# VectorE in place of TensorE for turning two weight matrices: WV ahead of step 0, Wo within it

## The reference, cut to what matters

```python
x = x + (x @ W.T + adapter_b(x @ A_b.T))          # layer 0, adapter by sequence
x = x + einsum('bct,bcd->bdt', x, w1[idx1])       # layer 1, mixes tokens
# layer 2, attention
q, k, v = x @ Wq.T, x @ Wk.T, x @ Wv.T            # per head of 32; q scaled by beta
attn = softmax(where(causal, q @ k.T / sqrt(32), min))
x = x + (attn @ v) @ Wo.T
x = x + einsum('bct,bcd->bdt', x, w3[idx3])       # layer 3, mixes tokens
```

## Time and profile before

| | us |
|---|---|
| median of 3 runs | 619.65 (619.6 to 620.12) |
| the profiled execution | 619.72 |
| its span, first to last instruction | 618.0 |
| TensorE busy in the span | 604.5 (98%) |
| VectorE busy | 386.8 (63%) |
| ScalarE busy | 225.0 (36%) |
| GpSimd busy | 109.7 (18%) |

### The profile page before, as it was taken

The page is one execution under the profiler, slowest core; times in us unless marked ns, Lnnn a source line. Parts: engine busy times, 40 slices in busy tenths (PEclk is TensorE's granted clock), DMA queues, the critical chain, the costliest instruction groups (busy, mean ns, idle before and its releaser), DMA issues.

```text
span 618.0 us, 21481 instructions
## 1 busy us (share of the span) xinstructions
PE 604.5 (98%) x8534; PEld 522.7 (85%) x8534; DVE 386.8 (63%) x561; ACT 225.0 (36%) x434; POOL 109.7 (18%) x101
## 2 busy tenths in 40 slices
PE   6999999899999999999999999999999999999998
PEld 5897979789898888989888898988989788898885
DVE  3569676565766756576675757666575765637374
ACT  4534533242434425143342514435152442413222
POOL 2004030120303003030310303021030302203030
PEclk9999999899999999999999999999999999999999
DMA  8541313222232222223222222323223222220212
GB/s 276 168 146 48 90 43 83 73 50 70 72 88 72 60 72 63 72 76 93 68 64 72 62 74 72 76 74 79 72 57 79 72 64 73 60 73 5 69 41 103
DMA packets 62104, 48.29 MB, mean 78 GB/s; under 512 B 16826, under 2 KB 47546, under 8 KB 62074
## 3 DMA queue, kind: packets, MB, share of 16 engines
q1 hardware_dynamic: 58122, 41.84, 24.9%
q10 hardware_dynamic: 3952, 6.03, 2.9%
HBM read 30.54 MB, written 17.30 MB: 77 GB/s over the span
## 4 chain that ended last, share of the span: by engine, by line
PE 95%; DVE 1%; DMA 1%; issue 1%; ACT 1%; ACTq 0%; DVEq 0%
PE banks L617 10%; PE banks L622 10%; PE banks L618 10%; PE banks L645 5%; PE banks L716 5%; PE banks L717 5%; PE banks L723 5%; PE banks L647 5%; PE banks L649 5%; PE banks L557 5%; PE banks L559 5%; PE banks L561 5%; PE banks L670 4%; PE banks L662 4%; PE banks L686 3%; PE banks L601 3%
## 5 line engine op out<-in xcount | busy, mean ns | idle before, releaser
L617 PE MATMUL banks<-x1T_hi,w_hi 128*128 128x256 f32 x512 | 130.3, 287 | 0.2 <-ACT x_in L885 0.2
L618 PE MATMUL banks<-x1T_hi,w_lo 128*128 128x256 f32 x512 | 128.2, 283 | 0.0
L617 PEld LDWEIGHTS banks<-x1T_hi,w_hi 128*128 128x128 f32 x512 | 98.0, 191 | 0.8 <-ACT x_in L885 0.4
L618 PEld LDWEIGHTS banks<-x1T_hi,w_lo 128*128 128x128 f32 x512 | 98.1, 192 | 0.0
L1374 POOL TENSOR_TENSOR probs<-probs,row_max 128x1024 f32<-128x1024 f32 x32 | 61.0, 1906 | 123.5 <-DVE row_max L1176 123.5
L622 PE MATMUL banks<-x1T_lo,w_hi 128*128 128x256 f32 x512 | 82.2, 283 | 0.0
L1356 POOL TENSOR_TENSOR w_own<-w_in,own 128x128 f32<-128x128 f32 x32 | 14.7, 460 | 361.4 <-PE banks L584 267.4
L622 PEld LDWEIGHTS banks<-x1T_lo,w_hi 128*128 128x128 f32 x512 | 70.6, 192 | 0.0
L1162 DVE TENSOR_TENSOR qkT<-banks,beta 128x512 f32<-128x512 f32 x32 | 22.1, 690 | 61.7 <-PE banks L622 61.7
L885 ACT ACTIVATE x_y<-banks 128x512 f32<-128x512 f32 (+1 forms) x17 | 9.9, 584 | 128.8 <-PE banks L584 122.0
L1180 DVE TENSOR_REDUCE row_sum<-probs 128x16 f32<-128x1024 f32 x32 | 39.0, 1218 | 24.2 <-ACT probs L966 24.2
(11 more groups left out here) (133 smaller groups left out, 1055.3 us busy)
## 6 DMA issues: line engine op xcount, KB each, us to landing
x_rows<-x_in SPq DMA_DIRECT2D x64, 128.0 KB, 2.3
x_kept<-x_rows SPq DMA_DIRECT2D x16, 512.0 KB, 3.7
x_in<-in_x_dram SPq DMA_DIRECT2D x60, 128.0 KB, 2.8
out_dram<-x_y SPq DMA_DIRECT2D x15, 512.0 KB, 3.0
b_sel<-b_parts SPq DMA_DIRECT2D x180, 32.0 KB, 1.7
w_in<-in_L_cond_weights_dram SPq DMA_DIRECT2D x128, 16.0 KB
probsT<-in_L_cond_W_dram ACTq DMA_DIRECT2D x1, 1024.0 KB, 7.3
probs<-in_L_cond_Wk_dram ACTq DMA_DIRECT2D x1, 1024.0 KB, 5.9
```

The costliest lines, as they stand in the source:

```text
L617: nc.tensor.matmul(out_ap, w_hi[:, w, c, cols], x1T_hi[:, c, :], start=(c == 0), stop=False)
L618: nc.tensor.matmul(out_ap, w_lo[:, w, c, cols], x1T_hi[:, c, :], start=False, stop=False)
```

## The change

WV and WO are loaded in 32-row blocks with four DMAs each (`load_blocks`, rows of 512 bytes) and turned by VectorE (`turn_w(n)`, eight parts of 128x512) into a new SBUF tile `w_whole` of four parts. Parts 0 to 3 are WV, 4 to 7 WO. ACT copies a part to `w_hi` (`part_hi`), VectorE subtracts into `w_lo` (`part_lo`). TensorE's eight `turn_part` calls for them are gone, and it waits for `part_split` ahead of `values(0, 0)` (4) and of `scores(1)` (8). WV's load is issued after W0's parts and WO's after WV's part 2. In step 0, `query_part(0)` goes ahead of the keys. For WO's new layout `attend` writes head `4m+j` to partitions `32m` of chunk `j` (before, partitions `32j` of chunk `m`), with the two loops exchanged, in all steps.

```diff
+        w_whole = sb("w_whole", [P, NC, NC, P])
...
-                 WV: as_stage(probsT[:], "p t (c d) -> p (t c) d"),
-                 WO: x2_y[:].rearrange("p a t d -> p (a t) d")}
+                 WV: probsT[:].rearrange("p t n -> p (t n)").rearrange("p (b n) -> p b n", n=P),
+                 WO: x2_y[:].rearrange("p a t d -> p (a t d)").rearrange("p (b n) -> p b n", n=P)}
...
-        GROUPS_OF = {W0: range(0, 4), WK: range(6, 10), WQ: range(10, 14), WV: range(14, 18), WO: range(18, 22)}
-        ring = [0, 6, 7, 4, 5, 6, 7, 4, 5, 6, 0, 7, 6, 7, 6, 7, 6, 7, 0, 5, 6, 7]
+        GROUPS_OF = {W0: range(0, 4), WK: range(6, 10), WQ: range(10, 14)}
+        ring = [0, 6, 7, 4, 5, 6, 7, 4, 5, 6, 0, 7, 6, 7]
...
+        PARTS_V, PARTS_O = range(NC), range(NC, 2 * NC)
+
+        def matrix_part(w, n):
+            k = WV if n in PARTS_V else WO
+            return w[:, k, :, n % NC * P:(n % NC + 1) * P]
+
+        def whole_part(n):
+            return w_whole[:, n % NC]
...
             def attend():
                 for t in range(TILES):
-                    for m in range(NC):
+                    for j in range(JG):
                         for r in range(SEQT):
-                            for j in range(JG):
+                            for m in range(NC):
                                 at = j % 2 * BANK + (m // 2 * TILES + t) * P + m % 2 * S
                                 head = (JG * m + j) * HD
                                 last = nc.tensor.matmul(
-                                    attn_bank(r)[j * HD:(j + 1) * HD, m, t, :], v[half(r), t, head:head + HD],
+                                    attn_bank(r)[m * HD:(m + 1) * HD, j, t, :], v[half(r), t, head:head + HD],
...
+                    pe.wait_ge(part_split, len(PARTS_V))
...
                     pe.wait_ge(v_copied, TILES)
                     adapters_down(2)
-                    turn_part(WO, 0)
+                pe.wait_ge(x1_hi_done, TILES * (i + 2))
+
+                if not prev:
+                    query_part(0, split=TILES * 2)
                 pe.wait_ge(x1_copied, SEQT * i + 1)
-                pe.wait_ge(x1_hi_done, TILES * (i + 2))
                 for m in range(NC):
                     if m == 2:
                         pe.wait_ge(x1_copied, SEQT * (i + 1))
                     key_part(i + 1, m)
-                    if not prev and m > 0:
-                        if m == 1:
-                            pT_copied(0, HG)
-                        turn_part(WO, m)
-                if not prev:
-                    pe.wait_ge(turned_lo, GROUPS_OF[WO][0] + 1)
-                for m in range(NC):
+                for m in range(NC) if prev else range(1, NC):
                     if m == 2:
                         pe.wait_ge(k_copied_act, i + 2)
                     if m == (1 if parted(i) else 3):
                     pe.wait_ge(y_copied_act, i)
                     pe.wait_ge(y_copied_dve, i)
...
-                    pe.wait_ge(turned_lo, GROUPS_OF[WO][-1] + 1)
+                    pe.wait_ge(part_split, len(PARTS_V) + len(PARTS_O))
...
             turn_part(WQ, 3)
-            turn_part(WV, 0)
             pe.wait_ge(x1_hi_done, TILES)
             for m in range(NC):
                 key_part(0, m)
-                if m == 0:
-                    pe.wait_ge(tables_done, PSEQ)
-                else:
-                    turn_part(WV, m)
+            pe.wait_ge(tables_done, PSEQ)
             pe.wait_ge(turned_lo, GROUPS_OF[WQ][-1] + 1)
             for m in range(NC):
                 if m == 2:
                     pe.wait_ge(k_copied_act, 1)
                 query_part(m)
-            pe.wait_ge(turned_lo, GROUPS_OF[WV][-1] + 1)
             adapters_down(1)
...
+            def load_blocks(k, matrix):
+                for g in range(JG):
+                    act.dma_start(stage[k][g * SQ:(g + 1) * SQ],
+                                  matrix.rearrange("(b j) (g n) -> g j b n", j=SQ, g=JG)[g]).then_inc(w_loaded[k], 16)
...
                     xa_low_part(2)
-                    take_hi(GROUPS_OF[WO][0], w_hi[:, WO, 0, :])
+                    xa_hi_part(2)
+                    for n in PARTS_O:
+                        part_hi(n)
                     copy_k(1)
-                    for c in range(1, NC):
-                        take_hi(GROUPS_OF[WO][c], w_hi[:, WO, c, :])
-                    xa_hi_part(2)
                 if nxt2:
...
+            def part_hi(n):
+                act.wait_ge(part_turned, n + 1)
+                copy(matrix_part(w_hi, n), whole_part(n)).then_inc(part_hi_done, 1)
...
             take_matrix(W0)
+            load_blocks(WV, Wv)
             take_hi(GROUP_A, a_all[:, 0:2, :], in_chunks(bank_of_group(GROUP_A))[:, 0:2, :])
...
             copy(xa_first_hi, xa_first).then_inc(xa_first_hi_done, 1)
-            load_w(WV, Wv)
             for c in range(3):
                 take_hi(GROUPS_OF[WK][c], w_hi[:, WK, c, :])
+                part_hi(c)
+            act.wait_ge(xa_first_split, 1)
+            load_blocks(WO, Wo)
             x0_copy(0)
             take_hi(GROUPS_OF[WK][3], w_hi[:, WK, 3, :])
             take_hi(GROUPS_OF[WQ][0], w_hi[:, WQ, 0, :])
...
             take_hi(GROUPS_OF[WQ][3], w_hi[:, WQ, 3, :])
-            load_w(WO, Wo)
-            take_hi(GROUPS_OF[WV][0], w_hi[:, WV, 0, :])
+            part_hi(3)
             x_hi(1)
-            take_hi(GROUPS_OF[WV][1], w_hi[:, WV, 1, :])
             copy_k(0)
-            for c in (2, 3):
-                take_hi(GROUPS_OF[WV][c], w_hi[:, WV, c, :])
             act.wait_ge(turned_lo, GROUP_A + 1)
...
-                    for c in range(NC):
-                        if c == NC - 1:
-                            copy_k(1)
-                        take_lo(GROUPS_OF[WO][c], w_lo[:, WO, c, :], w_hi[:, WO, c, :])
+                    for n in PARTS_O:
+                        turn_w(n)
+                    for n in PARTS_O:
+                        part_lo(n)
+                    copy_k(1)
                 if nxt2:
...
+            def turn_w(n):
+                k, first = (WV, PARTS_V[0]) if n in PARTS_V else (WO, PARTS_O[0])
+                if n == first:
+                    dve.wait_ge(w_loaded[k], 16 * JG)
+                if k == WO:
+                    dve.wait_ge(part_split, n - NC + 1)
+                blocks = stage[k][:, NC * (n - first):NC * (n - first + 1), :]
+                nc.vector.transpose(
+                    whole_part(n).rearrange("p c (b j) -> p b c j", j=SQ),
+                    blocks.rearrange("p b (e c) -> p b c e" if k == WV else "p b (c e) -> p b c e", c=NC))\
+                    .then_inc(part_turned, 1)
+
+            def part_lo(n):
+                dve.wait_ge(part_hi_done, n + 1)
+                rest(matrix_part(w_lo, n), whole_part(n), matrix_part(w_hi, n)).then_inc(part_split, 1)
...
                 take_lo(GROUPS_OF[WK][c], w_lo[:, WK, c, :], w_hi[:, WK, c, :])
+                turn_w(c)
             x0_copy(0)
...
             dve.wait_ge(tables_done, PSEQ)
-            take_lo(GROUPS_OF[WV][0], w_lo[:, WV, 0, :], w_hi[:, WV, 0, :])
+            turn_w(3)
             turn_x(1)
-            for c in (1, 2):
-                take_lo(GROUPS_OF[WV][c], w_lo[:, WV, c, :], w_hi[:, WV, c, :])
+            for n in PARTS_V:
+                part_lo(n)
             copy_k(0)
-            take_lo(GROUPS_OF[WV][3], w_lo[:, WV, 3, :], w_hi[:, WV, 3, :])
             x_lo(1)
             scale_q(0)
             sum_xa(1)
```

More of the change, by code:

```diff
@@ L196, in cond_resid_kernel @@
         tables_done = sem("tables_done")
+        part_turned = sem("part_turned")
+        part_hi_done = sem("part_hi_done")
+        part_split = sem("part_split")
         xT_mm = sem("xT_mm")
@@ L285, in attn_of @@
         def attn_of(ap, r):
-            return ap.rearrange("p m (t b s) -> p b m t s", t=TILES, b=SEQT)[:, r]
+            return ap.rearrange("p j (t b s) -> p b j t s", t=TILES, b=SEQT)[:, r]
         def attn_bank(r):
-            return bank[AT[r]].rearrange("p (m t s) -> p m t s", m=NC, t=TILES)
+            return bank[AT[r]].rearrange("p (j t s) -> p j t s", j=NC, t=TILES)
         def own_blocks(r):
@@ L324, in last_attn @@
         def last_attn(ap, t, r):
-            return ap.rearrange("p m (t b s) -> p m t b s", t=TILES, b=SEQT)[:, :, t, r]
+            return ap.rearrange("p j (t b s) -> p j t b s", t=TILES, b=SEQT)[:, :, t, r]
         def last_attn_bank(t, r):
-            return bank[SC[TILES * t + r]][:, 0:PT].rearrange("p (m s) -> p m s", m=NC)
+            return bank[SC[TILES * t + r]][:, 0:PT].rearrange("p (j s) -> p j s", j=NC)
         HALF_D = D // 2
+        PARTS_V, PARTS_O = range(NC), range(NC, 2 * NC)
[4 more added lines that the diff above has]
+            return w_whole[:, n % NC]
         block = ctx.enter_context(nc.Block())
@@ L489, in pieces_of @@
             def pieces_of(k, dc):
-                if k != WO:
-                    return [every_fourth(stage[k][:, oc, :], dc) for oc in range(NC)]
```

(8 more changed lines are left out.)

## The result

Measured beside each other: the kernel after 626.83 us (median of 4 runs, 623.11 to 629.43), before 619.62; ratio 1.0123, 95% interval 1.0095 to 1.0152. The same source measured again gave 626.23 beside 619.79. The forecast was 621.8, the range ended at 624.6: the sign was right, the loss was 7 us, not 2.

What follows compares the result with a forecast made beforehand. TensorE was taken as the bound, busy 604.5 of 618.0 us, so its new waits are paid in full. Terms -1.9 + 4.6 + 1.4 - 1.9 = +2.2 gave 621.8 us, range 620.0 to 624.6.

Steps and rivals of the forecast that it cites:

- term 1: Prologue: TensorE no longer turns WV's four parts, 0.48 us each; -1.9 us.
- term 2: Prologue: `first_layer1` waits for ScalarE's copy of x0, starting at 30.3 in place of 25.73; +4.6 us.
- term 3: Behind the prologue's gap: TensorE's clock falls to the lower level for a stretch; +1.4 us, bounds 0 and 3.4.
- term 4: Step 0 to step 1's values: WO's parts off TensorE, query 0 ahead of the keys; -1.9 us, or -0.8 with slow turns.
- bound 21.8: Prologue: start of VectorE's first WV turn if the queues share badly; 21.0 was taken, not before 20.8.
- a lap: Prologue chain: one turn, ScalarE's parts of WV and WK, and VectorE's subtraction; 2.8 us.
- the issues: Prologue chain: ScalarE's four DMA issues for WO ahead of its copy of x0; 1.8 us.
- two stretches: Within rival "More is paid" (22%, 623 to 624.8): two stretches at the lower clock after the gap, +1.8 us more.
- the clock stays up: Rival, 15%: no clock loss behind the prologue's gap, terms 1, 2 and 4 alone; +0.8, 620.5 us.
- faster: Rival, 13%: TensorE's shorter program removes the 2.0 us stop in step 1's `scores` with its clock stretch; 618.1 us.
- The exchanged loops of `attend` (0): `attend` in all 16 steps: the loops only trade places, at no cost; 0 us.

Runs made afterwards that it cites:

- after_again: The kernel after, unchanged, measured again: 626.23 us beside before's 619.79, ratio 1.0108.
- decoupled: Kernel after with ScalarE's WV copies and Wo's load behind WQ's last part, VectorE turning parts 2 and 3 later: 620.32 us, before 619.79, ratio 1.0023.
- v_only: Before with only WV turned by VectorE, ScalarE's copies of it behind those of x0; Wo and `attend` as before: 618.33 us, before 618.68, ratio 0.9992.
- gap_only2: Before with 12 scratch copies on ScalarE ahead of its copy of x0, into a tile behind all others: 626.68 us, before 619.79, ratio 1.0109.
- after_warm: Kernel after with 33 turns of the identity on TensorE where it waits for ScalarE's copy of x0: 622.63 us, before 618.68, ratio 1.0064.
- decoupled_pad: The decoupled kernel with 66 instructions that wait for what has come, ahead of TensorE's first work: 626.0 us.

## Why the prediction was wrong

The failure is not in one term. The profile of after_again is the best one to take the median loss apart with, since its 626.38 is near both medians. Against the profile of before, in us:

| | forecast | after_again |
|---|---|---|
| WV's parts (term 1) | -1.9 | -1.9 |
| start of layer 1 (term 2) | +4.6 | +6.0 |
| clock between layer 1 and first scores (term 3) | +1.4 | +2.25 |
| first scores to step 2's scores (term 4) | -1.9 | -0.3 |
| from there to the end | 0 | +0.7 |
| sum | +2.2 | +6.7 |

So term 4 is off by 1.6, term 2 by 1.4, term 3 by 0.9, and a stop in the last step that was put at nothing adds 0.7. All four miss to the same side. Term 3 is read as what the way from layer 1 to first scores (18.54) has more than in decoupled (16.29), which had no stretch there.

**Term 1 (-1.9 for WV's parts): right.** From layer 1 to the first scores the profiles show 18.21 us in before, 16.28 in v_only and 16.29 in decoupled.

**Term 2 (+4.6): right chain, too small.** 5.3 in the first profile, 6.0 in the second. The first turn started at 21.15, 21.6 and 22.56 in three profiles (taken: 21.0; bound 21.8), a turn took 1.1 for 1.0, a lap 2.9 for 2.8, the issues 1.94 for 1.8. Nearly each was taken at its low end, and I summed them as if they were centred. Over all eight profiles that turn WV in this way, without pads ahead of TensorE's work, the first turn starts between 21.15 and 22.61, in four of them behind 21.8, the latest that was allowed for. That bound was too tight.

**Term 3 (+1.4): right size of a stretch, wrong count.** The size of one stretch was right: layer 1 to first scores took 17.60 in after, that is 16.29 + 1.3; in after_again, with two stretches, 18.54, that is + 2.25. What failed is the count. I had one stretch in the trace of before, took the gap to cause one more, and gave "two stretches" to a rival. The runs of after lose 4.0 us to the lower clock on the mean, those of before 1.0, with ten of 23 runs at none. gap_only2 shows that a gap alone is enough for it (five runs at 0.992, 5.0 us; two stretches at the gap and one behind the stop in step 2's scores). With less idle time less is lost: 2.0 us on the mean in after_warm, and decoupled_pad, with 2.6 us idle at this place, had no stretch there. But decoupled's run at 0.989 is not accounted for. The rival "the clock stays up" fell: in no run of after did it. That rule of the Trainium skill ("TensorE: Matmul & The Clock Gate", "Why this matters for your kernels") pointed the right way; its price had to come from runs.

**Term 4 (-1.9): right on the turns, wrong on the gain; the largest miss.** WO's turns took 0.666 us and WV's 1.10: skipping in SBUF costs, as argued, and the wait for `k_copied_dve` is 0.8 (forecast 0.75). But first scores to step 2's scores take 69.40 us in after for 69.59 in before, a gain of 0.2. With the code back at its place (after_warm) it is 68.43, a gain of 1.16, and in v_only, with Wo on TensorE, 69.57, none. So Wo's turns are worth 1.16 of the 1.9, and some 1.0 of that was lost again to the stop in step 1's scores, where the forecast had none: this is the step that failed here. The 0.8 left of the 1.9 went in five delays of 0.14 to 0.17 us that the forecast didn't have, none of them large: ahead of step 0, behind the stop for `x1T_lo`, at the wait for the last keys, in query 1, and from `attend` to the values.

**The stop that moves.** The rival "faster" had seen that the program gets shorter ahead of the stop, and the forecast decided that it would stay as it was. It stayed in step 2 (33 products on) and two others came with it. The one in the last step, up to 2.4 us, was on no list. That these stops are TensorE waiting for code is inferred: their place follows the length of the program ahead of them in all seventeen profiles, and nothing of data ends them. The Trainium skill ("Runtime: NRT & Kernel Launch", "Instruction fetch mechanics") calls the cost of crossing from one block of code to the next "mostly hidden" in straight code. If the stops are such crossings, they were not hidden here: 1.5 to 2.2 us once a run, in the middle of 128 products that follow one another, and more often when the program shifted.

**The exchanged loops of `attend` (0): right.** A loop step takes 36.42 us in after, 36.40 in before; 15 of these 0.02 are 0.3 us at most.

**The sum again.** Profiled: -1.9 + 5.3 + 1.3 - 0.2 = +4.5, which is 118.04 - 113.53. Behind step 2's scores 1.1 came back (the span is 3.4 longer), since this execution's stop there had no lower clock behind it, as before's had. The typical run has what the profile of after_again shows: gap 0.7 more, 0.9 more of clock in the prologue, a second place with a stretch at the lower clock (behind the stop in step 2's scores, at 122 us), and 0.7 in the last step; its span is 624.6, 6.7 above before's (618.0). What share of the 7 us the last step's stop has in the median isn't settled, as only profiled runs show it.

## What to carry to other kernels

Where TensorE is the bound, an idle gap costs its length and then the clock behind it: count the stretches at the lower clock over several runs, not in one trace; a gap of 5 us cost 7 here (gap_only2). Where runs come with and without such a stretch, compare those with the same number of them: this showed v_only's gain of 1 us, which the medians hid. Before moving a matrix's preparation to another engine, follow what that engine owes TensorE next, and put the new work behind it (decoupled: 6 us less than after, with the same instructions). A chain of many terms, each taken at the end of its bounds that looks likeliest, comes out late, not on the mean. And a change that shortens a program can move stops that nothing of data explains, into places where there were none.

## What the runs showed of the hardware

The place of tiles in SBUF changes the pace of TensorE's key and query products: one unused tile of 24,000 B ahead of x_in or of x1T, no instruction changed, gives 613.0 and 612.0 us for 618.7 and 619.6. The version with it is faster than both kernels. Why, and which address decides, stays open: 8,192 and 16,384 B bring nothing.

Waits on a semaphore that has been reached aren't free on TensorE: 132 such waits, in 66 instructions, held it until 8.95 us where after's first work began at 4.48, so at least 4.5 us, 68 ns for each instruction. How much of it is the wait itself and how much the loading of 66 more instructions isn't taken apart.

A stop put down to "issue" moves with the place of the code: 66 instructions fewer ahead of it moved it by 33 products and brought 0.6 to 0.9 us in one step and, in four profiles of five, 0.7 to 2.4 in another.

VectorE turns 128x512 numbers of SBUF in 0.666 us when it reads them in order and in 1.10 when it reads every fourth.
